# Cross-attention projection: the first pair's queries and keys loaded beside the last blocks, context loads one block earlier, query and state pieces moved by a block

## The reference, cut to what matters

```python
q = (query @ Wq + bq).reshape(B, Nq, H, D).transpose(0, 2, 1, 3)       # 16 heads of 16
k = (key_value @ Wk + bk).reshape(B, Nkv, H, D).transpose(0, 2, 1, 3)
v = (key_value @ Wv + bv).reshape(B, Nkv, H, D).transpose(0, 2, 1, 3)
attn = softmax(clip(einsum('bhqd,bhkd->bhqk', q, k) * scale, -CLAMP, CLAMP))
x = einsum('bhqk,bhkd->bqhd', attn, v).reshape(B, Nq, Cq) @ Wo + bo
```

## Time and profile before

| | |
|---|---|
| time, median of 3 runs | 1091.82 us (1088.47 to 1094.22) |
| profiled execution: span from its first to its last instruction | 1089.9 us |
| projection stage in it, to the last value copy of DVE | 0 to 137.0 us |
| first instruction of the heads stage after the barrier | 139.2 us |
| first score matmul of the heads stage | 145.7 us |
| PE, DVE, ACT, POOL busy over the span | 934.1, 822.0, 650.3, 303.0 us |
| mean granted clock of TensorE | 0.912 of full |

### The profile page before, as it was taken

The page is one execution under the profiler, slowest core; times in us unless marked ns, Lnnn a source line. Parts: engine busy times, 40 slices in busy tenths (PEclk is TensorE's granted clock), DMA queues, the critical chain, the costliest instruction groups (busy, mean ns, idle before and its releaser), DMA issues. The chain is left out here.

```text
span 1089.9 us, 20914 instructions
## 1 busy us (share of the span) xinstructions
PE 934.1 (86%) x7702; PEld 582.8 (53%) x7716; DVE 822.0 (75%) x1716; ACT 650.3 (60%) x1045; POOL 303.0 (28%) x332
## 2 busy tenths in 40 slices
PE   6997948999999999999688997767877778899877
PEld 5976814444444444444364884553455556744545
DVE  5776679989999999992244896999878777369267
ACT  3432405878787888877344443339999998511212
POOL 1000078889900000000120452003646453000021
PEclk9998957999999999999889998767699999898979
DMA  6868662232323223320212224720065224771000
GB/s 195 306 236 294 224 156 64 74 85 75 80 75 82 74 76 79 81 52 1 64 56 88 58 59 110 180 70 1 26 180 147 59 59 132 234 190 64 1 1 20
DMA packets 99320, 111.83 MB, mean 103 GB/s; under 512 B 26658, under 2 KB 75730, under 8 KB 99218
## 3 DMA queue, kind: packets, MB, share of 16 engines
q1 hardware_dynamic: 98578, 109.89, 34.7%
q10 hardware_dynamic: 640, 0.59, 0.2%
HBM read 80.95 MB, written 29.43 MB: 101 GB/s over the span
## 5 line engine op out<-in xcount | busy, mean ns | idle before, releaser
L854 ACT ACTIVATE pT<-bank 128x512 f32<-128x512 f32 x512 | 278.4, 597 | 93.6 <-PE bank L771 72.2
L876 DVE TENSOR_REDUCE rmax<-bank 128x2 f32<-128x1024 f32 x256 | 307.3, 1223 | 26.7 <-PE bank L739 25.8
L783 PE MATMUL bank<-pT,V 128*17 128x256 f32 x2048 | 161.0, 386 | 4.7 <-ACT oT L860 4.6
L1757 PE MATMUL bank<-K1s,qs 97*128 97x512 f32 x256 | 112.7, 544 | 34.6 <-ACT work L1881 16.5
L771 PEld LDWEIGHTS bank<-qs,ks 49*128 49x128 f32 x1024 | 77.7, 186 | 112.3 <-ACT pT L854 98.8
L771 PE MATMUL bank<-qs,ks 49*128 49x256 f32 x1024 | 129.9, 332 | 2.3 <-ACT pT L854 0.5
L739 PE MATMUL bank<-ks,qs 49*128 49x512 f32 x512 | 110.6, 427 | 16.6 <-DMA ks<-k_parts_d 9.4
L2046 POOL TENSOR_TENSOR total<-total,work 128x1024 f32<-128x1024 f32 x40 | 95.0, 2381 | 31.2 <-ACT work L1881 30.4
L1757 PEld LDWEIGHTS bank<-K1s,qs 97*128 97x128 f32 x256 | 53.2, 219 | 52.2 <-issue 37.5
L1941 DVE MAX8 cand<-work 128x8 f32<-128x128 f32 x384 | 76.4, 277 | 0.0
L783 PEld LDWEIGHTS bank<-pT,V 128*17 128x17 f32 x2048 | 34.5, 95 | 63.2 <-ACT pT L854 42.8
(11 more groups left out here) (464 smaller groups left out, 1809.4 us busy)
## 6 DMA issues: line engine op xcount, KB each, us to landing
k_parts_d<-kparts SPq DMA_DIRECT2D x48, 512.0 KB
ks<-k_parts_d SPq DMA_DIRECT2D x381, 64.0 KB, 2.2
K1s<-k_parts_d SPq DMA_DIRECT2D x96, 128.0 KB
cn<-in_ctx SPq DMA_DIRECT2D x32, 384.0 KB, 3.5
cx<-in_ctx SPq DMA_DIRECT2D x16, 384.0 KB, 5.0
w<-in_L_ffn_w SPq DMA_DIRECT2D x32, 128.0 KB, 2.4
w2e<-in_L_ffn_w SPq DMA_DIRECT2D x16, 128.0 KB, 2.9
W<-in_L_xattn_W SPq DMA_DIRECT2D x2, 1024.0 KB, 8.0
```

Source lines behind the costliest of these rows:

```text
L783: t = pe.matmul(bank[32 * c:32 * c + VW, 7, a * S:(a + 1) * S], V[:, b * NCH + 4 * g + c, h, :], pT[:, (at + 2 * (c // 2) + a) % 8, c % 2 ...
L854: p_made.up(act.activation(pT[:, at % 8, :], bank[:, 4 + at % 3, :], ACT.Exp))
L876: max_read.up(dve.tensor_reduce(rmax[p % 2][:, :, qt, c], bank[:, b0:b0 + 2, :], AX.X, ALU.max))
L1757: m = pe.matmul(bank[:, b0 + c, :], qs1[0:NROW1, b * H1 + h, q], K1s[h][0:NROW1, keys], start=True, stop=(what == "new"))
```

## The change

It does three things, all in the projection stage and at the start of the next one.

1. **Context loads.** The load of block n + 3 instead of n + 2 stands at the start of SP's turn n. It waits until PE has transposed block n + 1, at the start of PE's turn n. The load of block 2 stands ahead of the loop.
2. **Query and state pieces.** PE's second query tile moves from turn 6 to turn 7, DVE's split of it from turn 7 to turn 8. PE's and ACT's state pieces move from turns 11 and 12 to 12 and 13, DVE's last from turn 13 to 14. DVE's state pieces of turns 8 to 11 stay.
3. **First pair.** SP issues the loads of the first pair's queries (2 DMAs), of the ones for `ks0` (2) and of the first pair's keys (4 quarters of 6) in its turns 11 to 14, ahead of the stores of these turns: ten DMAs in turn 11, six in each of 12, 13 and 14. They first wait until all queries and the keys of blocks 0 to 7 have landed. The wait at the end of the projection for the last stores goes; SP makes it after the barrier, ahead of the second pair's loads. ACT has no DMA in the heads stage any more. `ks0` and the three `qs` get places in SBUF that are free during the projection, and some buffers of the projection change places.

```diff
+    heads_base = spot[0]
+    ks = [sb("ks0", [P, S2], F32R)]
+    spot[0] = LATER + 2 * 4 * LB * 32 * 4
+    qs = [sb(f"qs{j}", [P, S], F32R) for j in range(3)]
...
 def keys_sync():
...
+        def first_pair(k):
+            if k == 0:
+                sp.wait_ge(*q_stored.at(16 * (1 + 4 * NSTK)))
+                sp.wait_ge(*ones_made.at(1))
+                for j in range(2):
+                    sp.wait_ge(*kparts_out[j].at(48 * (NBB // 2)))
+                load_pair_queries(sp, 0)
+                load_key_ones(sp, 0)
+            for a in range(2):
+                load_key_parts(sp, 0, a, k)
+
+        load(2)
         for n in range(NBLK):
-            if n + 2 < NBLK:
-                load(n + 2)
+            if n + 3 < NBLK:
+                load(n + 3)
+            if FIRST <= n < FIRST + 4:
+                first_pair(n - FIRST)
...
-        for j in range(2):
-            sp.wait_ge(*kparts_out[j].at(48 * (NBLK // 2)))
-        sp.wait_ge(*q_stored.at(16 * (1 + 4 * NSTK)))
...
 def keys_scalar():
-            if n in (11, 12):
+            if n in (12, 13):
                 next(s4, None)
...
 def keys_vector():
-            if n in (6, 7):
-                query(n - 6)
-            if n in (8, 9, 10, 11, 13):
+            if n in (6, 8):
+                query(n // 2 - 3)
+            if n in (8, 9, 10, 11, 14):
                 next(s4, None)
...
 def keys_tensor():
-            if n in (5, 6):
-                queries(n - 5)
-            if n in (11, 12):
+            if n in (5, 7):
+                queries(n // 2 - 2)
+            if n in (12, 13):
                 next(s4, None)
...
 def heads_sync():
-        load_queries(0)
-        load_key_parts(sp, 0, 0, 0)
-        for q in range(1, 4):
-            load_keys(0, q)
+        for j in range(2):
+            sp.wait_ge(*kparts_out[j].at(48 * (NBLK // 2)))
         load_queries(1)
+        load_key_ones(sp, 1)
         for q in range(4):
             load_keys(1, q)
...
 def heads_scalar():
-        for j in range(2):
-            if j:
-                load_key_parts(act, 0, 1, 0)
-            for a in range(2):
-                r = HALF_P * a + MAX_ROW
-                kones_in[j].up(act.dma_start(ks[j][r:r + 1, :].rearrange("p (a n) -> p a n", a=8).bitcast(F32),
-                                          ones[0:1, :].rearrange("p (a n) -> p a n", a=1).to_broadcast([1, 8, 512])), 16)
```

More of the change, by code:

```diff
@@ L299, in build @@
     V = sb("V", [P, NB * NCH, H0, VW])
+    heads_base = spot[0]
+    ks = [sb("ks0", [P, S2], F32R)]
+    spot[0] = LATER + 2 * 4 * LB * 32 * 4
+    qs = [sb(f"qs{j}", [P, S], F32R) for j in range(3)]
+    assert spot[0] <= END - 2 * S2 * 4
+    spot[0] = heads_base
+    kones_in = [flag(f"kones_in{j}") for j in range(2)]
+    key_in = [[flag(f"key_in{j}{q}") for q in range(4)] for j in range(2)]
+    query_in = [flag(f"query_in{j}") for j in range(3)]
+    kparts_out = [flag(f"kparts_out{j}") for j in range(2)]
+    q_stored = flag("q_stored")
     phase_begins()
@@ L302, in build @@
     wraw1, wraw2 = sb("wraw1", [P, NW]), sb("wraw2", [P, NW])
+    wq = sb("wq", [P, 2, D])
+    qf = sb("qf", [P, T])
+    qparts = sb("qparts", [P, 2, 2, T], F32R)
+    kparts = [sb(f"kparts{j}", [P, 3, 2, BLK], F32R) for j in range(2)]
     w1h, w1l, w2h, w2l = (sb(n, [P, NW], F32R) for n in ("w1h", "w1l", "w2h", "w2l"))
@@ L312, in build @@
     c2 = [sb(f"c2_{j}", [P, BLK], F32R) for j in range(2)]
-    kparts = [sb(f"kparts{j}", [P, 3, 2, BLK], F32R) for j in range(2)]
     q_stack_d = nc.dram_tensor("q_stack_d", [NH, NROW, S], F32).ap()
@@ L324, in build, with load_key_parts, load_key_ones, load_pair_queries @@
     pad_made = flag("pad_made")
-    kparts_out = [flag(f"kparts_out{j}") for j in range(2)]
+    HALF_P = P // 2
+    FIRST = 11
     WEIGHTS = (("L0_xattn_Wk", 0, D), ("L0_xattn_Wv", D, D), ("L1_xattn_Wk", 2 * D, P))
+    def load_key_parts(queue, p, a, q):
+        cols = slice(q * 1024, (q + 1) * 1024)
+        n = 2 * p + a
+        for r0, kp, qp in STACK:
+            key_in[p % 2][q].up(queue.dma_start(ks[p % 2][HALF_P * a + r0:HALF_P * a + r0 + D0, cols].bitcast(F32),
+                                                k_parts_d[n * D0:(n + 1) * D0, kp, cols]), 16)
+    def load_key_ones(queue, j):
+        for a in range(2):
+            r = HALF_P * a + MAX_ROW
+            kones_in[j].up(queue.dma_start(ks[j][r:r + 1, :].rearrange("p (a n) -> p a n", a=8).bitcast(F32),
+                                           ones[0:1, :].rearrange("p (a n) -> p a n", a=1).to_broadcast([1, 8, 512])), 16)
+    def load_pair_queries(queue, p):
+        for a in range(2):
+            query_in[p % 3].up(queue.dma_start(qs[p % 3][HALF_P * a:HALF_P * a + NROW, :].bitcast(F32),
+                                               q_stack_d[2 * p + a]), 16)
     def keys_sync():
@@ L561, in build @@
     phase_ends()
-    NP_, HALF_P = NH // 2, P // 2
+    NP_ = NH // 2
     G = 8
@@ L567, in build @@
     LEAD = 5
-    ks = [sb(f"ks{j}", [P, S2], F32R) for j in range(2)]
-    qs = [sb(f"qs{j}", [P, S], F32R) for j in range(3)]
+    spot[0] += S2 * 4
+    ks.append(sb("ks1", [P, S2], F32R))
     pT = sb("pT", [P, 8, 2 * S])
```

20 lines of the change are left out of this document (4 added, 16 removed).

## The result

The changed kernel takes 1082.8 us (median of 6 runs, 1078.06 to 1083.95), the kernel before 1092.07 us in the same series (6 runs, 1088.47 to 1096.91). The ratio is 0.9908 with a 95% interval of 0.9883 to 0.9933: 9.3 us faster, 7 to 13 us. The forecast was 17.7 us faster, 1074.1 us, with a range of 1069 to 1081. The direction was right and the size was about twice what came.

A forecast was written before the change was run, and what follows sets the result against it. PE was taken to bound the projection, with gaps and lowered clock, and DVE the heads stage's start. Savings 1.5 + 6.0 + 4.1 + 1.7 + 4.4 = 17.7 us; 1091.8 - 17.7 = 1074.1 us, range 1069 to 1081.

The forecast's parts named there:

- The three waits: PE's projection gaps: 3.5 us for a context load, 2.6 for DVE's wch, 1.5 for DVE's qf; all were to go.
- thin cover: Projection: block 13's load lands at 96.7 us and PE wants it at 97.8, a cover of 1.1 us.
- The cover of 5 us or more: End of the projection: loads of blocks 14 and 15 come 5 us or more before PE wants them.
- DVE's lag: Projection turn 8: moved query and state pieces put DVE 1.4 us behind; cost taken as 0, other bound 1.4 us.
- The clock in these terms: Projection turns 10 and 12: low clock after PE's gaps goes too, saving 2.5 and 1.5 us.
- it waits for DVE (137.04) and no longer for SP: Barrier at the projection's end: heads stage starts at 137.5 us instead of 139.19, saving 1.7 us.
- The 4.4 us: Heads stage start: first score matmul comes 2.1 us after the stage's start instead of 6.5.
- SP becomes the bound: Rival, 0.03: key-part issues cost 1.19 us, SP falls 20.6 us behind in turns 11 to 14, kernel takes 1097 us.
- The heads stage should only slide: Heads stage: clock stays low at its start as before, so work behind the first matmul is unchanged and only starts earlier.
- as long as PE falls idle at all: Heads stage start: any idle gap throttles the clock, so 3.4 instead of 9.4 us gains nothing beyond itself.
- a returned stall: Rival, 0.20: block 13's load or turn 11's key stores miss their slack by 1 to 3 us; 1078.5 us.
- The 3 us that it gave to the later stages' clock: Forecast's own range, 1071 to 1077: up to 3 us from DVE's lag and how the later stages' clock falls.

The follow-up runs named there:

- e10 a: The changed kernel word for word, run again for a second trace: 56.0 us from the first score matmul to the first copy of oT.
- e10 b: The changed kernel word for word, run again for a third trace: 52.3 us from the first score matmul to the first copy of oT.
- e8: The changed kernel with the first pair's key bytes in half as many DMAs, in SP's turns 11 and 13 only: 1077.35 us, ratio 0.9861.
- e3: The kernel before with part 1 (earlier context loads) alone: 1087.22 us, ratio 0.9938.
- e14: The kernel before, unchanged, run again for a second trace: 52.4 us from the first score matmul to the first copy of oT.
- e1: The changed kernel with part 3 undone, parts 1 and 2 kept: 1083.77 us, ratio 0.9904.
- e2: The changed kernel with parts 1 and 2 undone, so part 3 alone: 1089.67 us, ratio 0.9949.
- e11: The changed kernel with the first pair's loads behind, not ahead of, the key stores in SP's turns 11 to 14: 1079.65 us, ratio 0.9864.
- e6: The changed kernel with first-pair loads moved to SP's turns 3, 4, 6, 7 and 12, ks0 in a place of its own: 1077.14 us, ratio 0.9863.
- e12: The kernel before with extra, unread 128-row matmuls around the start of the heads stage: 1094.88 us, ratio 1.0014.
- e13: The changed kernel with extra, unread 128-row matmuls around the start of the heads stage: 1079.36 us, ratio 0.9886.
- e5: The changed kernel with extra, unread matmuls around the start of the heads stage, 49-row ones behind score steps: 1092.87 us, ratio 1.0007.
- e9: e6 with extra, unread bf16 matmuls of 128 rows around the start of the heads stage: 1073.6 us, ratio 0.9805.
- e7: e6 with the extra, unread matmuls of e5: 1091.14 us, ratio 0.9978.

## Why the prediction was wrong

**Parts 1 and 2 up to PE's last product: right.** The three waits are gone, turns 9 to 12 take 6.6 to 7.0 us, and PE saved 12.3 us in the first pair of traces, where 11.6 were forecast (10.8 in the average of three traces each). The load of block 13 kept its thin cover in the first trace and missed it by 0.4 us in e10 a. The cover of 5 us or more that the forecast gave to block 15 was wrong: SP's backlog delays this load, and PE waited 0.9, 0.2 and 1.2 us for it in e10 a, e10 b and e8. That DVE's lag costs nothing was right too. The clock in these terms (2.5 and 1.5 us) is less firm than the forecast had it: in e3 a gap of 2.62 us cost no clock, and in e14 a wait for the next load stood in place of the 2.5 us. The parts alone saved 8.0 and 6.2 us up to the first matmul.

**Part 3: the step that failed is "it waits for DVE (137.04) and no longer for SP".** The prediction had SP's last stores untouched and costed the 28 added issues only against ACT's need of a free buffer. It did see a backlog: it put the key stores of turn 11 at 100 to 102 us, up to 4.2 us past the end of PE's turn 11 at 97.8. By its own figures SP then needs at most 6.2 us in turn 12 and 5.5 in turns 13 and 14, which hold no context load any more, against 6.65 us of PE. So SP would have caught up by 2.8 us or more of the 4.2 and been free before the tiles of turn 15 are ready. What was wrong is the size of the issue: 0.42 us, from the quiet heads stage, where turns 12 to 14 took 0.60, 0.74 and 0.72 on average. SP's turns 12 to 14 took 6.8, 6.6 and 6.5 us, as long as PE's, and nothing was caught up. At 0.42 us the 18 issues would have taken 7.6 us and not 12.3 (an estimate from these rows), and SP would have reached its last stores 4.8 us sooner, ahead of the tiles that they store. Besides, the last three stores took 4.0 us and not 1.7.

The first matmul came at 132.03 us, 4.1 us later than forecast: DVE's last value copy is 1.3 us late, since ACT waits for stores to land (which the forecast had called hidden), and the stage begins 3.3 us behind that copy and not 0.5. The 4.4 us from the stage's start to the first matmul came as forecast. e1 (part 3 is worth 1.7 us beside the others), e2 (5.3 us alone) and e11 (SP alone holds the barrier) show that it is SP's queue, and e6, where the first matmul comes at 127.8 us, shows that the rest of the step was sized rightly. How much is the count of issues and how much the bytes is settled only in part: half the issues gave 2.5 us (e8), most loads moved ahead of turn 12 gave 4.2 (e6). Why an issue takes longer in these turns is open; the runs show only that it does so where the DMA share is high.

The rival "SP becomes the bound" named the mechanism. It was priced only for the longest issue of the rows and was said to decide from 0.67 us on; the issues came to lie just there.

**"The heads stage should only slide": right as a mechanism, wrong as a number for one trace.** Another 3.6 us between the first matmul and the first `oT` came from the clock's return. Three traces of each kernel, the moments of return over 13 traces and the pair e12 and e13 show that this is chance: with the clock held at 1.00 both kernels take 48.7 us there. The forecast was made against a single trace of before whose first pair was 2.8 us shorter than in the next two. That the later traces of both kernels still differ by some 1.8 us on average (52.3 and 52.4 against 52.3 and 56.0) is within this scatter, and two traces each don't say more.

**The clock at the start of the heads stage.** By the Trainium skill (TensorE: Matmul & The Clock Gate, Part 1) the clock is throttled by default and activity releases it. The forecast drew from it only that a shorter gap is worth nothing beyond itself, and the trace agrees: the clock is at 0.50 at the first matmul again. The forecast's "as long as PE falls idle at all" goes further than the traces do: the clock stayed at 1.00 over the gaps of 2.62 us in e3 and 3.47 us in e14. Taken as "a busy PE keeps its clock" the rule does not hold here: PE of e5 is busy in all of the 6 us from 141 to 147 while the clock falls to 0.50.

**The range** ended at 1081, 1.8 us too low. It took a returned stall and SP's backlog as rivals of which only one could hold. The 3 us that it gave to the later stages' clock stood beside the forecast alone and not on top of a rival, and here the two came together.

## What to carry to other kernels

A queue that is late has two readers: the engine that waits for its buffers, and the barrier at the end of the stage. Carry the backlog through to the last instruction of the queue before calling its cost nothing, and take the issue time from a stretch in which the DMA engines are as full as they will be, as an average: here the median did not move and a few long issues made the difference.

Loads for the next stage belong where the queue has pauses, as early as their data and a free place allow, and not beside the last stores (e6: 4.2 us up to the first matmul).

Before a forecast rests on one trace, look for the times in it that depend on when the granted clock comes back. If a stage starts with matmuls of few rows behind a bound of another engine, some of 128 rows in PE's idle time can be worth trying (e6 to e9: 3.5 us between the medians of two series, with intervals that overlap, and 3.6 us in the first pair of the traces). They are not free: on the kernel before (e12) the medians show no gain.

## What the runs showed of the hardware that was not expected

- Matmuls of 49 rows back to back did not keep the clock: it fell from 1.00 to 0.50 some 6 and 5 us into them with PE busy throughout (e5 and e7). With three bf16 matmuls of 128 rows behind each step it stayed at 1.00 through the first pair (e9, e12, e13).
- After the maxima PE is busy nearly all the time at 1.2 GHz, and in the kernels without extra matmuls the clock came back between 31 and 46 us behind the first matmul, at moments that differ between traces of one kernel. The first pair took from 49.6 to 56.0 us by it.
- Behind one and the same gap of PE (3.5 us, turn 9 of the kernel before) the clock fell to 0.50 in the first trace and stayed at 1.00 in e14.
- The issue of one and the same load on SP took 0.42 us in a quiet stage and 0.60 to 0.74 us on average where the DMA share was 0.84 to 1.00 (0.9 in turn 12 of e6), by a few issues of up to 1.3 us; three stores took 4.0 instead of 1.7 us.
